# First attention: the order of TensorE's scores and of VectorE's normalising

## The reference

```
mod = silu(c) @ ada_w.T + ada_b                     # shift, scale, gate per sequence
h = layernorm(x) * (1 + scale) + shift
q, k, v = split(h @ qkv_w.T + qkv_b)                # 16 heads of 16
attn = softmax(where(mask, q @ k.T * 0.25, -1e9))   # 64 x 64 per sequence and head
x = x + gate * ((attn @ v) @ proj_w.T + proj_b)
x = x + gate_mlp * mlp(modulate(layernorm(x)))      # 256 -> 1024 -> 256, gelu
```

## Time and profile before

| | |
|---|---|
| median of 3 runs | 2479.66 us (2479.55 to 2481.01) |
| the profiled execution's own time | 2483.42 us |
| its span | 2481.6 us |
| TensorE busy | 2349.0 us, 95% |
| VectorE busy | 1906.0 us, 77% |
| ScalarE busy | 1552.9 us, 63% |
| GpSimd busy | 1038.9 us, 42% |
| first attention, last P V on TensorE | starts at 462.87 us |
| mean granted clock of TensorE | 0.964 of full speed |

### The profile page before, as it was taken

One profiled execution on the slowest core, in us unless ns is written; L12 is line 12 of the kernel. 1 busy time (PEld: TensorE's weight loads), 2 busy tenths in 40 slices (PEclk: granted clock), 3 DMA queues, 4 the chain that ended last, 5 costly groups with the idle time before them and its releaser, 6 DMA issues. The chain is left out here.

```text
span 2481.6 us, 67114 instructions
## 1 busy us (share of the span) xinstructions
PE 2349.0 (95%) x24912; PEld 2077.4 (84%) x24912; DVE 1906.0 (77%) x3763; ACT 1552.9 (63%) x2982; POOL 1038.9 (42%) x939
## 2 busy tenths in 40 slices
PE   7999999999999899999999999999999727999997
PEld 5888888799999788888888888888888626999996
DVE  6999999776666688888888888888888686666663
ACT  5888888766666465656556565655656454556553
POOL 4888888400000143434434344343434203445543
PEclk8999999999999899999999999999999856999998
DMA  4111110110110100000000000000000122333423
GB/s 142 39 38 42 38 39 27 49 33 21 32 32 21 37 14 16 15 17 13 17 13 17 17 13 17 13 17 13 17 17 13 36 38 70 91 92 84 96 50 34
DMA packets 78720, 89.21 MB, mean 36 GB/s; under 512 B 18480, under 2 KB 72496, under 8 KB 76080
## 3 DMA queue, kind: packets, MB, share of 16 engines
q1 hardware_dynamic: 66352, 71.10, 9.2%
q0 software_dynamic: 12288, 17.05, 4.2%
HBM read 62.42 MB, written 25.69 MB: 36 GB/s over the span
## 5 line engine op out<-in xcount | busy, mean ns | idle before, releaser
L1275 POOL TENSOR_TENSOR a_rq<-a_vq,minus_half 128x8 f32<-128x8 f32 x256 | 417.6, 1641 | 97.9 <-DVE a_vq L1299 97.9
L1222 ACT ACTIVATE a_sq<-a_bqk 128x512 f32<-128x512 f32 x256 | 152.8, 597 | 351.3 <-PE a_bqk L126 351.3
L1270 POOL TENSOR_TENSOR a_rstd<-a_veps,minus_half 128x1 f32<-128x1 f32 x63 | 34.8, 552 | 580.4 <-DVE a_veps L1346 580.4
L124 PE MATMUL a_bqk<-wqk_hi,a_h_lo 128*128 128x512 f32 x512 | 207.6, 405 | 3.5 <-DVE a_h_lo L1315 3.5
L126 PE MATMUL a_bqk<-wqk_hi,a_h_hi 128*128 128x512 f32 x512 | 201.2, 393 | 0.0
L125 PE MATMUL a_bqk<-wqk_lo,a_h_hi 128*128 128x512 f32 x512 | 201.0, 393 | 0.0
L1291 DVE TENSOR_TENSOR a_qk<-a_bqk,a_rq 128x512 f32<-128x512 f32 x256 | 175.9, 687 | 29.8 <-POOL a_rq L1275 29.7
L1899 ACT ACTIVATE e_u<-e_bu,e_b 128x512 f32<-128x512 f32 x128 | 88.3, 690 | 157.1 <-PE e_bu L126 155.2
L2041 DVE TENSOR_TENSOR e_u_lo<-e_u,e_u_hi 128x512 fp32r<-128x512 f32 x128 | 88.9, 695 | 127.1 <-ACT e_u_hi L1904 126.4
L1207 ACT COPY a_vs<-a_ba 64x512 f32<-64x512 f32 x256 | 148.8, 581 | 53.6 <-PE a_ba L126 48.9
L1283 DVE TENSOR_REDUCE a_ss<-a_sq 128x8 f32<-128x512 f32 x256 | 173.7, 679 | 2.7 <-ACT a_sq L1222 1.0
(11 more groups left out here) (329 smaller groups left out, 8057.0 us busy)
## 6 DMA issues: line engine op xcount, KB each, us to landing
a_qk<-gates_of_rows SPq DMA_DIRECT2D x32, 256.0 KB, 4.3
tokens<-a_xs SPq DMA_DIRECT2D x64, 128.0 KB, 1.7
out<-a_xs SPq DMA_DIRECT2D x64, 128.0 KB, 1.7
e_w<-in_fc1s SPq DMA_DIRECT2D x8, 1024.0 KB, 5.0
e_w<-in_fc2s SPq DMA_DIRECT2D x8, 1024.0 KB, 4.8
a_gate<-gates_of_rows SPq DMA_DIRECT2D x122, 64.0 KB, 2.5
X<-in_x SPq DMA_DIRECT2D x56, 128.0 KB, 2.1
wst<-in_qkv_w SPq DMA_DIRECT2D x16, 128.0 KB, 2.5
```

Of the source, the lines that this page charges most:

```text
L124: tensor.matmul(to, w_lo, x_hi, start=start, stop=False)
L1222: nc.scalar.activation(sq[:, n * BK:(n + 1) * BK], b_qk[:, n * BK:(n + 1) * BK], ACT.Square).then_inc(s["sq"], 1)
L1275: nc.gpsimd.tensor_tensor(rq[:, 8 * n:8 * n + 8], vq[:, 8 * n:8 * n + 8], g.mhalf[:, 0:8], ALU.pow).then_inc(s["rq"], 1)
```

## The change

On TensorE the scores' block (line 761 and after: its waits for `kbd`, `q_out` and `shifted`, and its matmuls) moves from behind xhat's turn to the place right behind P V, ahead of the second half of the probabilities. On VectorE the low part of the output (tile i-6) and reciprocal and normalising (tile i-5) move from the head of the step to the place behind the statistics of x, right ahead of the mask, maximum and shift of the scores. No instruction is added or dropped, and no wait is changed.

```diff
@@ vector, step
-                if has(-6):
-                    dve.wait_ge(s["o_hi"], i - 5)
-                    nc.vector.tensor_tensor(o_lo[:, :, :], b_pj[:, D:2 * D].rearrange("p (c q) -> p c q", c=DC),
-                                            o_hi[:, :, :].bitcast(F32), ALU.subtract).then_inc(s["o_lo"], 1)
-                if has(-5):
-                    dve.wait_ge(s["o"], i - 4)
-                    heads = b_o[:, 0:H * HV].rearrange("p (h d) -> p h d", d=HV)
-                    nc.vector.reciprocal(rs[:, :], heads[:, :, HD0]).then_inc(s["recip"], 1)
-                    dve.wait_ge(s["recip"], i - 4)
-                    if has(-6):
-                        dve.wait_ge(s["oT"], i - 5)
-                    nc.vector.tensor_tensor(o_sb[:, :].rearrange("p (h d) -> p h d", h=H), heads[:, :, 0:HD0],
-                                            rs[:, :].unsqueeze(2).to_broadcast([P, H, HD0]), ALU.mult)\
-                        .then_inc(s["normed"], 1)
                 if has(2):
...
+                if has(-6):
+                    dve.wait_ge(s["o_hi"], i - 5)
+                    nc.vector.tensor_tensor(o_lo[:, :, :], b_pj[:, D:2 * D].rearrange("p (c q) -> p c q", c=DC),
+                                            o_hi[:, :, :].bitcast(F32), ALU.subtract).then_inc(s["o_lo"], 1)
+                if has(-5):
...
                 if has(-2):
                     dve.wait_ge(s["s"], i - 1)
@@ tensor, step
                     last.then_inc(s["o"], 1)
+                if has(-2):
+                    pe.wait_ge(s["kbd"], i - 1)
+                    pe.wait_ge(s["q_out"], i - 1)
+                    if has(-3):
+                        pe.wait_ge(s["shifted"], i - 2)
+                    pe.sem_inc(s["pe_held"], 1)
+                    for c in range(DC):
+                        for r in range(2):
+                            feats = slice(r * S, (r + 1) * S)
+                            for b in range(2):
+                                at = turn % 2 * P + b * S
+                                toks = slice(b * S, (b + 1) * S)
+                                last = nc.tensor.matmul(b_s[toks, r * 512 + c * 256:r * 512 + (c + 1) * 256],
+                                                        qT[feats, (turn - 2) // 2 % 2, c, at:at + S],
+                                                        kbd[feats, c, :, toks], start=True, stop=True)
+                    last.then_inc(s["s"], 1)
                 if has(-4):
                     pe.wait_ge(s["pT_out"], 2 * (i - 4) + 1)
                     turn_probs(1)
@@ tensor, step, behind xhat's turn
                     last.then_inc(s["xT"], 1)
-                if has(-2):
-                    pe.wait_ge(s["kbd"], i - 1)
...
-                    last.then_inc(s["s"], 1)
                 if has(-6):
                     pe.wait_ge(s["o_lo"], i - 5)
```

More of the change, by code:

```diff
@@ L583, in step @@
                     nc.vector.tensor_tensor(gates[:, :], b_o[:, :], gbias, ALU.add).then_inc(s["gate_out"], 1)
+                if has(-6):
[3 more added lines that the diff above has]
+                if has(-5):
+                    dve.wait_ge(s["o"], i - 4)
+                    heads = b_o[:, 0:H * HV].rearrange("p (h d) -> p h d", d=HV)
+                    nc.vector.reciprocal(rs[:, :], heads[:, :, HD0]).then_inc(s["recip"], 1)
+                    dve.wait_ge(s["recip"], i - 4)
+                    if has(-6):
+                        dve.wait_ge(s["oT"], i - 5)
+                    nc.vector.tensor_tensor(o_sb[:, :].rearrange("p (h d) -> p h d", h=H), heads[:, :, 0:HD0],
+                                            rs[:, :].unsqueeze(2).to_broadcast([P, H, HD0]), ALU.mult)\
+                        .then_inc(s["normed"], 1)
                 if has(-2):
```

## The result

| | before | after |
|---|---|---|
| median | 2479.61 us (2478.47 to 2481.01, 4 runs) | 2529.58 us (2526.88 to 2532.95, 4 runs) |
| ratio to before | | 1.0201, 95% interval 1.0189 to 1.0214 |
| the profiled execution's own time, its span | 2483.42, 2481.6 us | 2528.65, 2526.9 us |
| a step of the first attention | 6.60 us | 7.45 us, each fourth one 7.54 |
| first matmul of the MLP stage starts at | 467.62 us | 513.60 us |

A forecast was written before the change was run, and what follows sets the result against it. TensorE's own queue was taken to set the 6.60 us step. 56 steps of + 0.86 us (48.2) with the stage's start and end terms gave + 49.8 us, so a median of 2529.5 us, range 2512 to 2546.

The forecast's parts named there:

- The wait uncovered at V: V product waits for ScalarE's hT once scores leave; turn to V 1.89 us, only 0.16 us saved there.
- The extra 0.12 us in the loop: ScalarE starts hT 0.54 us behind xhat's turn in the steady loop, against 0.42 in the start-up.
- The scores' slot: On TensorE, scores cost 1.02 us put in behind P V; taking them out behind xhat's turn frees 1.21 us.
- The step and its number: First attention's step goes from 6.60 to 7.46 us, + 0.86 in each of 56 steps, 48.2 us.
- The ends of the stage: Steps 2 and 3 add 2.4 us, step 4 adds 0.2; steps 61 to 63 and the stage's end, - 1.
- A: Rival at the V product: no wait for hT, only the shorter scores' slot counts, - 11 us, 2469 us; chance 0.06.
- B: Rival: scores behind P V wait for the previous tile's shifted scores, 84 us more, 2564 us; chance 0.07.
- C: Rival: idle time in each step lowers TensorE's clock to 1.2 GHz through the stage, + 300 us; chance 0.03.
- 1.00 at three quarters busy: Near the stage's end TensorE is 4.50 of 6.00 us busy at granted clock 1.00, cited against the lower-clock rival.
- D: Rival: a longer turn of VectorE or ScalarE sets the step and hides the loss, time unchanged; chance 0.01.
- VectorE's order: VectorE's moved instructions are the same ones and cost 0; VectorE doesn't set the step.

The follow-up runs named there:

- E4: Changed kernel with each chunk of hT written by one activation of 128 columns instead of two of 64: 2500.39 us, 1.0081 of the kernel before.
- E3: Changed kernel with xhat's turn also moved ahead of the q or k product on TensorE: 2466.23 us, 0.9953 of the kernel before.
- E2: Kernel before with only the change's VectorE half, TensorE's order as before: 2480.79 us, 1.0002 of the kernel before.
- E1: Kernel before with only the change's TensorE half (scores moved), VectorE's order as before: 2534.83 us, 1.0215 of the kernel before.
- E5: E3 with VectorE's order of the kernel before, so the two TensorE moves alone: 2469.84 us, 0.9959 of the kernel before.

## Why the prediction was right

**The wait uncovered at V.** The step that made the forecast, and it held in kind and size: a wait of 0.80 to 0.88 us in each step, 1.88 us from turn to V (forecast 1.89) and 0.23 to the second matmul. E4 shows that the way to hT sets the step, E3 that a cover of 2.1 us takes the wait away. The extra 0.12 us in the loop is there too: the written-out steps of the start-up, as the one at 63.04 us, have 1.77 us, as in the earlier trace rows, and 7.33 us a step:

```profile
63.04 0.38 PE L774 MATMUL a_bvx<-consts_sb,a_xhat 128*128 128x128 f32 x2
63.46 1.29 ACT L382 ACTIVATE a_hT<-a_bvx,shift_msa,scale_msa 128x64 f32<-128x64 f32 x4 [1.01 <-PE a_bvx L774]
64.81 0.39 PE L124 MATMUL a_bvx<-w_parts,pair_lo 128*128 128x256 f32 x1 [0.68 <-ACT a_hT L382]
```

**The scores' slot.** 1.02 us put in, 1.21 taken out: the first is measured in the timeline after (1.03), the second follows from E3, whose step is 6.60 - 6.41 = 0.19 us shorter.

**The step and its number.** 7.45 us forecast as 7.46. I had missed that each fourth step, where ScalarE's loop turns over, takes 0.09 us more. From the turn of step 4 to that of step 60 the kernel before takes 369.9 us and the one after 418.5: + 48.6 against 48.2.

**The ends of the stage.** These terms were off, and they are small. From the first turn to that of step 4 + 1.6 us (forecast 2.6). This term can't be judged to 1 us: E2, with TensorE's order of before, takes 34.3 us there and the kernel before 35.5. From the turn of step 60 to the MLP's first matmul 50.3 became 47.4: - 3.0 (forecast - 1). Part of it is that TensorE's waits at the second half of the probabilities, 4.0 us in the earlier trace rows, fell to 2.2; from 466.3 to 513.6 us:

```profile
PE a_bpt L694 <- ACT a_late L348: 2.2, 1, 2.2
```

The rest isn't broken down. Besides, the first turn, which waits for a load, came 1.2 us earlier in this execution. In all the stage ends 46.0 us later, not 49.8, and the profiled execution took 2528.65 us where the sum said 2533.2. The medians differ by 50.0 us; the changed kernel's four runs lie 6 us apart, and in E1, where the clock stayed low for longer, the end of the stage took 3.9 us more. So that the median was met to a tenth is luck; the mechanism and the step are not.

**The rivals.** A would have been right with a cover: E3 is the kernel it describes, at 2466 us against its 2469. B fell as argued, the scores didn't wait in the steady loop. C: in the loop the clock stayed at 1.00 with a busy share of 89%. But the row that the prediction set against C, 1.00 at three quarters busy, was too thin: the next six microseconds of the same trace of the kernel before are

```profile
455.00:461.00 6.00, 5.09 (x52) 4.44 (x52) 5.79 (x9) 4.64 (x9) 2.14 (x2) 0.72 0.33 91
```

so the clock did fall right behind that stretch, as it does at the stage's end in every run here. That row was no evidence against C; the 400 us of the loop at 1.00 are. D, that something else would hide the loss, fell too. VectorE's order, costed at nothing, is worth nothing that can be measured with either of TensorE's orders, old (E2) or new (E1), and some 5 us of the stage in E5.

## What to carry to other kernels

When one engine's queue is full, look for what each of its waits has in front of it: an instruction that is moved away may be the cover of a wait that it has nothing to do with. Count from the release that starts the other engine's work to the instruction that needs it, and compare with what is left between the two. Where two moves each uncover something, try them together before both are dropped; and where an order wins by a little, recompute the slack of the engines behind: 0.2 us of it was none here, since 0.25 us passed from VectorE's end to TensorE's start.

## What the runs showed of the hardware

A pause stands where TensorE's matmuls change between the full array and a part of it. In the scores' old place they start 0.20 us behind the last transpose, where two transposes are 0.11 us apart, and behind them the projection's second matmul comes 0.22 us behind its first, where 0.12 is usual. These 0.09 and 0.10 us are what the new place saves. The Trainium skill, "TensorEngine Tiling (Array Packing)", section "Tiling Modes", has the rule that a change of mode drains the array. With P V and scores side by side one such change is saved, and the measured 0.19 us a step agree. No run shows the drain itself.

Release from ScalarE to TensorE: the last of hT's four activations starts 1.42 us behind the turn in the loop of the changed kernel and 1.30 in its written-out steps 2 to 7, and V's first matmul 0.46 us after that start in both. The first activation starts 0.42 us behind the turn in these written-out steps, 0.54 in the loop and 0.63 in each fourth step of the loop; the cause of this wasn't tried.
